# Fifteen weight maxima of expert 1 at other slots of unit 1, and one of two maxima moved out of unit 0

## The reference

```
h = layernorm(x) * (1 + cb) + sb
probs = softmax(h @ Wr);  top-2 experts per token, first 320 per (batch entry, expert) kept
hid = relu(buf[e] @ W1[e] + b1[e])      # 512 -> 2048
y   = hid @ W2[e] + b2[e]               # 2048 -> 512
out = sum over the two experts of y * prob;   x = x + gb * out
```

## Time and profile before

| what | value |
|---|---|
| median of 3 runs | 2179.6 us (2177.0 to 2181.94) |
| the profiled execution | 2178.7 us |
| its span, first to last instruction | 2177.0 us |
| mean granted clock of TensorE | 0.998 |
| busy, share of the span: PE, DVE, ACT, POOL | 98%, 75%, 48%, 17% |

### The profile page before, as it was taken

How to read it: one execution, slowest core, us unless ns; L and a number is a source line. 1 busy time by engine, 2 the same in 40 slices (tenths; PEclk the granted TensorE clock), 3 DMA queues, 4 the chain that set the end, 5 groups by cost and what they waited for, 6 DMA issues and landing times.

```text
span 2177.0 us, 33797 instructions
## 1 busy us (share of the span) xinstructions
PE 2142.3 (98%) x12574; PEld 1187.1 (55%) x12574; DVE 1639.9 (75%) x2901; ACT 1042.8 (48%) x2050; POOL 377.2 (17%) x335
## 2 busy tenths in 40 slices
PE   8999999999999999999999999999999999999997
PEld 2454454544564655556464655556464655656464
DVE  7899999999887887487568758765875887487351
ACT  5565676665462644356153525524461544356050
POOL 1134344343333010100101010110101010000101
PEclk9999999999999999999999999999999999999999
DMA  8899995775756545344534534452444345343301
GB/s 287 245 265 249 230 263 135 186 185 114 176 177 155 160 122 150 78 112 117 140 91 117 148 90 120 112 145 74 104 137 118 94 130 149 80 102 98 44 6 25
DMA packets 353206, 300.94 MB, mean 138 GB/s; under 512 B 242476, under 2 KB 242732, under 8 KB 352529
## 3 DMA queue, kind: packets, MB, share of 16 engines
q1 hardware_dynamic: 331136, 256.63, 42.6%
q0 software_dynamic: 21904, 42.14, 10.2%
HBM read 163.84 MB, written 93.01 MB: 118 GB/s over the span
## 4 chain that ended last, share of the span: by engine, by line
PE 89%; DVE 4%; issue 1%; DMA 1%; POOL 1%; SPq 1%; ACT 1%; DVEq 0%; POOLq 0%; ACTq 0%
PE bank L2084 33%; PE bank L2010 31%; PE bank L1926 21%; PE bank L1875 1%; DMA reg_d<-in_w 1%; PE bank L1998 1%; POOL slot_rows L734 1%; PE bank L2063 0%; DVE reg_a L1641 0%; DMA reg_e<-reg_e 0%; PE bank L1886 0%; PE bank L1888 0%; SPq L503 0%; DVE reg_e L1280 0%; DVE reg_d L1641 0%
## 5 line engine op out<-in xcount | busy, mean ns | idle before, releaser
L2084 PE MATMUL bank<-reg_b,reg_c 128*128 128x512 f16 x3792 | 824.1, 379 | 3.7 <-DVE reg_e L1529 2.8
L2084 PEld LDWEIGHTS bank<-reg_b,reg_c 128*128 128x128 f16 x3792 | 370.5, 98 | 447.3 <-DVE reg_e L1529 5.0
L1926 PE MATMUL bank<-reg_c 128*128 128x512 f16 x2296 | 505.2, 379 | 1.3 <-ACT reg_e L888 1.3
L2010 PE MATMUL bank<-reg_e,reg_a 128*128 128x320 f16 x2880 | 447.6, 299 | 2.2 <-DVE reg_e L1600 2.2
L1926 PEld LDWEIGHTS bank<-reg_c 128*128 128x128 f16 x2296 | 222.1, 98 | 258.6 <-ACT reg_e L888 1.8
L2010 PEld LDWEIGHTS bank<-reg_e,reg_a 128*128 128x128 f16 x2880 | 280.8, 98 | 115.2 <-DVE reg_e L1600 2.5
L769 POOL DMA_INDIRECT out_dram<-reg_e,midx x79 | 142.8, 1807 | 1005.7 <-DVE reg_e L1533 879.6
L981 ACT ACTIVATE reg_e<-bank,b1s 128x320 f32<-128x320 f32 x120 | 63.3, 527 | 404.5 <-PE bank L2010 404.5
L2010 PE MATMUL bank<-reg_e,reg_d 128*128 128x320 f16 x1440 | 232.5, 299 | 0.0
L1529 DVE SCALAR_TENSOR_TENSOR reg_e<-bank,inv,reg_e 128x512 f32<-128x512 f32 x79 | 59.1, 748 | 223.5 <-PE bank L2084 223.5
L2010 PEld LDWEIGHTS bank<-reg_e,reg_d 128*128 128x128 f16 x1440 | 139.6, 98 | 57.8 <-ACT reg_e L981 4.3
(11 more groups left out here) (242 smaller groups left out, 2631.9 us busy)
## 6 DMA issues: line engine op xcount, KB each, us to landing
reg_d<-in_w SPq DMA_DIRECT2D x232, 512.0 KB, 4.1
slot_rows<-zrow SPq DMA_DIRECT2D x32, 516.0 KB, 4.7
reg_b<-in_x SPq DMA_DIRECT2D x16, 1024.0 KB, 6.9
out_dram<-reg_b SPq DMA_DIRECT2D x16, 1024.0 KB, 6.2
reg_d<-in_w SPq DMA_DIRECT2D x8, 1024.0 KB, 9.8
slot_rows<-zrow SPq DMA_DIRECT2D x32, 129.0 KB, 4.6
reg_d<-in_wmod SPq DMA_DIRECT2D x4, 1024.0 KB, 11.7
reg_e<-mod_rows SPq DMA_DIRECT2D x7, 512.0 KB, 4.3
```

What stands on the lines that cost most here:

```text
L1926: ins = mm(dst[:, :], wqs[:, ws, kc, e0:e0 + P], xns[:, j % 2, xs, kc, :], start=kc == 0 and xs == 0 and ws == 0, stop=kc == KC - 1 and ws ...
L2010: ins = mm(dst[:, 0:CAP], w[ws][:, c, p * P:(p + 1) * P], xs_of[:, KC * xs + 2 * i + c, j * CAP:(j + 1) * CAP], start=first and c == 0 and ...
L2084: ins = mm(bank_y[i % 2][:, :], hid[:, hs, hc, t * P:(t + 1) * P], w2s[:, ws, hc, :], start=k == 0 and hs == 0 and ws == 0, stop=k == HC - ...
```

## The change

Maximum 1 of W1 leaves the place ahead of unit 0's last output and becomes the first of fifteen between the pair steps of unit 1. Maxima 1 to 15 stand at the slots in `NEXT_MAX`. Before, maxima 2 to 7 stood at slots 4, 9, 14, 19, 24, 29 and maxima 8 to 15 at 35, 39, 43, 47, 51, 55, 59, 63. The head of W1's scale goes from slot 32 to 26, its tail from 52 to 44. No instruction is added or removed; the loads are the same and stand in the same order in SP's queue.

```diff
-W2_NEXT = 35
-W1_NEXT_HEAD, W1_NEXT_TAIL = 32, 52
+NEXT_MAX = (2, 5, 9, 13, 17, 20, 24, 28, 32, 35, 39, 43, 47, 50, 54)
+W1_NEXT_HEAD, W1_NEXT_TAIL = 26, 44
@@ pairs(v) of DVE
-                        if e == 0 and t >= W2_NEXT and (t - W2_NEXT) % 4 == 0 and (t - W2_NEXT) // 4 < 8:
-                            max_piece(1, 1, (t - W2_NEXT) // 4)
-                        if e == 0 and t % 5 == 4 and t // 5 < 6:
-                            max_piece(1, 0, 2 + t // 5)
+                        if e == 0 and t in NEXT_MAX:
+                            k = 1 + NEXT_MAX.index(t)
+                            max_piece(1, k // 8, k % 8)
@@ beside_outputs(e, u, t) of DVE, e == 0, u == 0
                     if t == 4:
-                        for k in range(2):
-                            max_piece(1, 0, k)
+                        max_piece(1, 0, 0)
```

## The result

| | before | change |
|---|---|---|
| median of the timed runs (7 and 7) | 2180.58 us | 2173.69 us |
| profiled execution, span | 2177.0 us | 2171.6 us |
| ratio of the runs, 95% interval | | 0.9971 [0.9961, 0.998] |

By the ratio the gain is 6.3 us of 2180 (interval 4.4 to 8.5); the two medians differ by 6.9 us. The forecast of 2175.6 us was 1.9 us too high, and the time lies inside its range. The time also lies past the line of 0.2% (2175.2 us), which had a chance of 0.42; staying short of it had 0.52. Two later comparisons of the same kernel gave 0.9971 [0.996, 0.9981] and 0.9972 [0.9963, 0.9981].

A forecast was written before the change was run, and what follows sets the result against it. PE, busy 98% of the span, bounds the kernel, so DVE edits pay only where PE waits. Terms -1.92 + 0.9 + 0 - 2.98 make -4.0 us: from 2179.6 to 2175.6 us, range 2172.4 to 2179.0 us.

The forecast's parts named there:

- First term: Start of unit 1: C11 of pair 0 starts at 701.75 instead of 703.67 us, so PE gains 1.92 us.
- Second term: Start of unit 1: maximum 3 waits for load 3 ahead of C22, giving back 0.9 us through R1 and P7.
- Rival 1: Start of unit 1: load 3 doesn't bind or lands sooner; gain 4.9 us, time 2174.7 us; chance 0.15.
- Third term: Unit 1's pairs: the fourteen further maxima, two to a period, fit PE's 5.70 us and cost 0.
- Rival 3: Unit 1's pairs: DVE can't keep the pace, C12 comes late to P5; 2184 us at 2.0 us per period; chance 0.05.
- Fourth term: Unit 1's second layer: the last maximum's load comes early, the chain runs as in unit 3, gaining 2.98 us.
- The margin that I read from unit 3: Second layer: output 2 ends at +40.05 us, tile 4 could begin at +40.14; each 0.1 us behind costs 0.1.
- waits A and B: PE's waits in unit 1: A at its start for C11, 2.37 us in all; B in its second layer, 2.8 us for an output.

The follow-up runs named there:

- second execution: The change run again without an edit, with a second profile: ratio to before 0.9971.
- experiment three: Against the change, maxima 1 to 3 moved to slots 5, 8, 12, behind the first combinations, and maxima 4 to 7 to 15, 18, 21, 24: ratio to before 0.9963.
- sixth experiment: Against the change, three maxima to a period (slots 2 to 37), head at 22, tail at 40: ratio to before 0.9985.
- seventh experiment: Against the change, maxima 1 to 3 at slots 5, 8, 12, then mostly every fourth slot, ending at 58; head 29, tail 48: ratio to before 0.9968.
- third execution: The change run once more without an edit, with a third profile: ratio to before 0.9972.
- experiment one: Against the change, maxima 2 to 15, head and tail put back in their old slots, so only maximum 1 moved: ratio to before 0.9995.
- experiments one to four: Edits of the change: old slots except maximum 1, 0.9995; maximum 1 back ahead of output, 0.9978; maxima 1-3 behind first combinations, 0.9963; maximum 15 at 63, 0.9979.

## Why the prediction was right, step by step

**First term, -1.92 us at C11: right, and too small in the profile of the change.** Load 1 came 3.00 us after unit 1's start and not 3.72, so nothing was left at C11 where I had left 0.45. In the second execution (4.23) PE waited 0.8 us there.

**Second term, +0.9 us for load 3: the mechanism is right, the size moves.** The profile shows 0.28 us of idle time at R1 and an excess of the whole first layer of 0.45 us (45.33 - 44.88, the undisturbed layer of experiment three), against my 0.9 + 0.45. Over three executions the excess of the first layer was 0.45, 1.03 and 1.92 us; my sum of the first two terms leaves 1.35, in the middle of them. That fits the landing that I took from the profile of before: 704.8 us is 7.91 us after unit 1's start, and the rule makes 44.94 + 7.91 - 6.48 = 46.37 us of it, where my two terms give 47.37 - 1.02 = 46.35. In the profile of the change load 3 landed 1 us sooner. Rival 1 (load 3 doesn't bind) is out: removing the load from C22's way brought the excess to zero each time.

**Third term, 0 for the denser train: right.** After the tail C12 came 0.1 us late, where I had allowed 0.4, and PE waited for none:

```profile
724.98 0.49 DVE L1623 SCALAR_TENSOR_TENSOR reg_e<-bank,reg_e 128x320 f32<-128x320 f32 x1 [0.54 <-PE bank L2008]
730.06 0.15 DVE L1162 TENSOR_SCALAR wmg<-wmg 128x1 f32<-128x1 f32 x1
730.80 0.49 DVE L1623 SCALAR_TENSOR_TENSOR reg_e<-bank,reg_e 128x320 f32<-128x320 f32 x1
736.39 0.49 DVE L1623 SCALAR_TENSOR_TENSOR reg_e<-bank,reg_e 128x320 f32<-128x320 f32 x1 [0.20 <-PE bank L2008]
```

Rival 3's place is confirmed by the sixth experiment. Its threshold (0.34 us per period over PE's 5.70, so 6.04) fits, as 6.18 us are past it, but no run stands near enough to it to measure it. Counted by full durations that period would be 7 x 0.48 + 3 x 1.21 = 6.99 us; it was 6.18. The prediction took only the first statement from the section "The DRAIN you can't avoid" of the Trainium skill's page "VectorE: DVE Perf Modes": the section goes on that an operation that isn't held starts earlier, and the operations in these rows do start earlier. So the section as a whole doesn't speak against the third term, and start to start is the count that came out.

**Fourth term, -2.98 us in the second layer: right to 0.01.** 55.77 became 52.78 us, in all three executions. The margin that I read from unit 3, 0.1 us, is as small as I said: in the seventh experiment 0.53 us of lateness of DVE at the end of the pairs cost 0.48.

**The sum.** Unit 1 gives -5.0 us between the first two profiles, and -4.7 between the means of two and three; forecast -4.0. The second layer makes -2.99 of it (forecast -2.98), the first layer -2.04 and -1.69 (forecast -1.02), so what unit 1 has beyond the forecast is when loads 1 and 3 landed. The timed runs say 6.3, and what lies between that and unit 1 is not settled.

One candidate is the stretch ahead of unit 1. Unit 1's start was 696.1 us in the mean of the change and 697.3 of before, and ahead of it both kernels do the same work. Before the third execution I had written that a start below 697 us would speak for something ahead of unit 1, and one above it for scatter. It came at 695.64 us, so by my own sign the change seems to have something there, though the first profile of before, at 696.89, also lies below that line. Scatter is not shown, and no mechanism is either.

The timed runs speak against chance alone as well. In all nine comparisons of kernels that have the denser slots, the timed gain is 1.0 to 2.4 us larger than what unit 1 gives against the mean of the two profiles of before; in experiment one, with the old slots, it isn't (1.1 against 1.2 us). But before against itself leaned the same way, by 0.0005 or 1.1 us, each interval is some 2 us wide to either side, and comparisons of one series share their runs of before. Another rival stays untested: waits A and B were profiled in two executions of before alone, and its runs spread further (2176.1 to 2184.7 us in the last series, the kernel of experiment three 2171.15 to 2172.74), so in executions without a profile they may be longer.

## What to carry to other kernels

An instruction that waits for a transfer delays all that stands behind it in an in-order engine (here C11 and C22 behind maxima 1 and 3): put what the busiest engine wants ahead of it, and the landing time, which moved by 1.5 us here, stops mattering. Where a chain ends on the last of many filler operations, look at what that end releases (here a load), and let the filler end early enough for its engine to have caught up too. How dense a filler may be follows from start-to-start times: two to a period fitted, three made DVE the pace.

## What was not expected of the hardware

Load 3 took 9.0 to 10.7 us from issue to landing in the eight profiles that recorded its landing, though 512 KB loads issued alone took 3.2 to 3.6: loads 1, 2 and 3 are issued in a row within 1.2 us. Most of the spread in wait A comes from when it is issued. And the part of the span in front of unit 1 varied from 695.6 to 701.7 us over twelve profiles, while the 1377 us behind unit 1 varied by 0.1 in eleven of them. The four starts at 699.98 us or later are those of experiments one to four, which ran on one chip, where the timed runs of before also took longer (2184.15 us, against 2180.17 and 2179.94 on the two other chips); the other eight starts lie within 2.2 us.
